# Second expert mixture: one bias product per tile of split weights in place of four bias products

## What is computed

```python
def _L1_ffn_ref(x, gate_w, expert_w, expert_b):
    gate_logits = jnp.einsum('bsd,ed->bse', x, gate_w)
    topk_vals, topk_idx = jax.lax.top_k(gate_logits, 2)
    weights = jax.nn.softmax(topk_vals.astype(jnp.float32), axis=-1)
    dense_w = jnp.sum(jax.nn.one_hot(topk_idx, E) * weights[..., None], axis=2)
    out = jnp.zeros(x.shape[:2] + (O,), dtype=x.dtype)
    for e in range(E):
        y_e = jnp.einsum('bsd,od->bso', x, expert_w[e]) + expert_b[e]
        out = out + dense_w[..., e:e + 1] * y_e
    return out

x = x + jnp.tanh(g_ffn[1]) * _L1_ffn_ref(_layernorm(x), gate_w, expert_w, expert_b)
```

## Time and profile before

| | us |
|---|---|
| median of three runs | 1305.46 (1303.05 to 1307.54) |
| the profiled execution | 1305.35 |
| its span in the trace | 1303.5 |
| TensorE busy | 1064.0 (82%) |
| VectorE busy | 840.9 (65%) |
| ScalarE busy | 545.8 (42%) |
| GpSimd busy | 530.7 (41%) |
| mean granted TensorE clock | 0.936 of full |

### The profile page before, as it was taken

The page is one execution under the profiler, slowest core; times in us unless marked ns, Lnnn a source line. Parts: engine busy times, 40 slices in busy tenths (PEclk is TensorE's granted clock), DMA queues, the critical chain, the costliest instruction groups (busy, mean ns, idle before and its releaser), DMA issues.

```text
span 1303.5 us, 32812 instructions
## 1 busy us (share of the span) xinstructions
PE 1064.0 (82%) x11717; PEld 826.4 (63%) x11717; DVE 840.9 (65%) x2315; ACT 545.8 (42%) x1065; POOL 530.7 (41%) x1053
## 2 busy tenths in 40 slices
PE   4898898994686488887888799999946569978898
PEld 2576676773576244444666577777734459977798
DVE  2565675765454689985666567777656666655475
ACT  2454465554454377664000023333311554346532
POOL 2454554654884888721101112222152224520261
PEclk8898898998798599998999899999968999989999
DMA  5321323411565554441000000000010530134331
GB/s 181 130 83 71 131 92 131 161 41 42 169 208 165 141 145 142 136 120 65 1 1 0 16 26 25 16 24 21 4 41 0 165 117 33 66 103 151 117 113 63
DMA packets 105787, 112.66 MB, mean 86 GB/s; under 512 B 12548, under 2 KB 95636, under 8 KB 104892
## 3 DMA queue, kind: packets, MB, share of 16 engines
q1 hardware_dynamic: 96732, 88.47, 21.6%
q0 software_dynamic: 8064, 22.06, 5.5%
q10 hardware_dynamic: 864, 0.43, 0.1%
HBM read 66.07 MB, written 44.84 MB: 85 GB/s over the span
## 4 chain that ended last, share of the span: by engine, by line
PE 58%; DVE 14%; issue 9%; ACT 7%; DMA 6%; POOL 5%; SPq 1%; DVEq 1%; ACTq 0%; POOLq 0%
PE psum L2677 5%; DMA PT<-xs 4%; PE psum L1082 3%; DVE mx L852 2%; PE psum L2392 2%; ACT PT L2335 2%; PE psum L1014 2%; ACT ext L2344 2%; POOL rstd L757 2%; PE psum L1065 2%; PE psum L1681 2%; PE psum L1016 2%; PE psum L1045 2%; PE psum L2377 2%; PE psum L1683 2%
## 5 line engine op out<-in xcount | busy, mean ns | idle before, releaser
L755 POOL TENSOR_SCALAR veps<-mv 128x1 f32<-128x1 f32 x112 | 27.2, 243 | 314.8 <-DVE mv L742 179.3
L852 DVE TENSOR_REDUCE mx<-psum 128x6 f32<-128x960 f32 (+3 forms) x80 | 80.7, 1009 | 68.7 <-PE psum L1050 67.4
L733 POOL DMA_INDIRECT got<-ys,rows_y x64 | 64.1, 1001 | 115.6 <-DMA ys<-yt 93.3
L939 ACT ACTIVATE PT<-psum 128x1024 f32<-128x1024 f32 x64 | 65.5, 1024 | 70.2 <-PE psum L1070 70.2
L2295 DVE TENSOR_REDUCE mx<-psum 128x4 f32<-128x1024 f32 x64 | 77.0, 1206 | 19.9 <-PE psum L2366 19.1
L2335 ACT ACTIVATE PT<-psum 128x1024 f32<-128x1024 f32 x64 | 65.5, 1023 | 34.6 <-PE psum L2377 34.3
L2677 PE MATMUL psum<-mskp,ident_r 128*128 128x512 f32 x256 | 71.3, 415 | 9.0 <-ACT PT L2630 8.6
L2106 DVE SCALAR_TENSOR_TENSOR x<-psum,cw,x 128x256 f32 (+1 forms) x128 | 53.0, 476 | 36.2 <-PE psum L2054 36.0
L1681 PE MATMUL psum<-xnTh,w7h 128*128 128x256 f32 x256 | 74.4, 291 | 1.2 <-issue 0.7
L1683 PE MATMUL psum<-xnTh,w7l 128*128 128x256 f32 x256 | 72.4, 283 | 0.0
L1682 PE MATMUL psum<-xnTl,w7h 128*128 128x256 f32 x256 | 72.4, 283 | 0.0
(11 more groups left out here) (414 smaller groups left out, 3425.2 us busy)
## 6 DMA issues: line engine op xcount, KB each, us to landing
xs<-qpad SPq DMA_DIRECT2D x17, 1024.0 KB, 5.1
PT<-xs SPq DMA_DIRECT2D x78, 128.0 KB, 2.1
ys<-yt SPq DMA_DIRECT2D x78, 128.0 KB, 2.1
ctxT<-in_ctxT SPq DMA_DIRECT2D x48, 128.0 KB, 2.3
ext<-qscr SPq DMA_DIRECT2D x96, 64.0 KB, 2.5
w_raw<-in_w SPq DMA_DIRECT2D x16, 384.0 KB, 3.3
arena<-in_w SPq DMA_DIRECT2D x4, 1280.0 KB, 10.1
q_parts<-kscr SPq DMA_DIRECT2D x66, 64.0 KB, 2.2
```

What stands on the lines that cost most here:

```text
L733: pool.indirect_dma_start(out=dst[:, t % 4, k], out_offset=None, in_=ys[:], in_offset=bass.IndirectOffsetOnAxis(ap=rows_y[:, t, k:k + 1], ...
L852: V.tensor_reduce(mx0[:, u0:u0 + m].rearrange("p j e -> p e j"), src, axis=AX.X, op=ALU.max, negate=True).then_inc(F("mx").sem, 1)
L939: A.activation(PT[:, 1024 * r:1024 * (r + 1)], bank(6, 2), ACT.Exp).then_inc(F("p").sem, 1)
```

## The change

The bias product leaves the groups: each group of a tile is six products. The bias of all eight experts, weighted, is one product per tile. For it GpSimd splits cw into three bfloat16 parts, each three times side by side (cwp, 72 columns, four instructions in `weight_parts`, issued behind the item's L755 and L757 and ahead of those of the next item). TensorE transposes cwp for both tiles into bank 6 after group 2, ahead of the router products; ScalarE copies it to cpT (72 rows by 256) between its two front copies and its tanh. After group 3 TensorE multiplies cpT by brows (72 rows by 256: for every pair of parts the bias of eight experts, in the first 256 columns of ebias) into bank 7, one product of 256 columns per tile. VectorE adds bank 7 to both tiles of x with one TENSOR_TENSOR of 512 columns, behind the last L2106 of the item and ahead of the router steps of the next. In stage 1 nine transfers of eight rows take the place of three transfers of one row.

```diff
+        pad_at = here()
         sb("pad", [128, 896])
+        cwp = over(pad_at, "cwp", [128, 2, 2, 9, TOP_E], BF16)
+        cwr = over(pad_at + 576, "cwr", [128, 2, TOP_E])
+        cpT = over(pad_at + 640, "cpT", [72, 2 * T], BF16)
+        brows = ebias[0:72, 0:C]
...
-                    pe.wait_ge(F("acc").sem, F("acc").at(b, 4 * j - 4))
+                    pe.wait_ge(F("acc").sem, F("acc").at(b, (-5, -1, 4, 8)[j]))
...
-                            MM(o, xl, wh, start=False, stop=False)
-                        t = MM(o, ones96[:], ebias[:, 512 * j:512 * (j + 1)], start=False, stop=True)
+                            t = MM(o, xl, wh, start=False, stop=(c == NC - 1))
                     t.then_inc(F("y").sem, 1)
+                    if j == 2:
+                        pe.wait_ge(F("mparts").sem, F("mparts").at(b, 4))
+                        plain(pe)
+                        for u in range(2):
+                            t = nc.tensor.transpose(bank(6).bitcast(BF16)[0:72, T * u:T * (u + 1)], cwp[:, s, u].rearrange("p c e -> p (c e)"), identb[:])
+                        t.then_inc(F("mxT_psum").sem, 1)
+                    if j == 3:
+                        pe.wait_ge(F("mxT").sem, F("mxT").at(b, 1))
+                        plain(pe)
+                        for u in range(2):
+                            t = MM(bank(7)[:, C * u:C * (u + 1)], cpT[:, T * u:T * (u + 1)], brows, start=True, stop=True)
+                        t.then_inc(F("pv").sem, 1)
...
+            def copy_weights(b):
+                act.wait_ge(f[3, "mxT_psum"].sem, f[3, "mxT_psum"].at(b, 1))
+                nc.scalar.copy(cpT[:], bank(6).bitcast(BF16)[0:72, 0:2 * T]).then_inc(f[3, "mxT"].sem, 1)
...
+            def weight_parts(n, s):
+                M = F("mparts")
+                two = cw[:, s]
+                pool.wait_ge(F("route").sem, F("route").at(n, ROUTE_STEPS[3] - 1))
+                plain(pool)
+                P.tensor_copy(cwp[:, s, :, 0:3], bc(two.unsqueeze(2), [128, 2, 3, TOP_E])).then_inc(M.sem, 1)
+                pool.wait_ge(M.sem, M.at(n, 1))
+                plain(pool)
+                P.tensor_tensor(cwr[:], two, cwp[:, s, :, 0], ALU.subtract).then_inc(M.sem, 1)
...
+            with pool.Fori(0, NB // 4) as i:
+                for s in range(2):
+                    for u in range(2):
+                        rs(i * 4 + (2 * s + u), 2 * s + u)
+                    weight_parts(i * 2 + s, s)
...
+                    if j == 3:
+                        dve.wait_ge(F("pv").sem, F("pv").at(b, 1))
+                        dve.wait_ge(acc.sem, acc.at(b, 16))
+                        nc.vector.tensor_tensor(x[:, bass.ds(2 * b, 2)] if not isinstance(b, int) else x[:, 2 * b:2 * b + 2], bank(7).rearrange("p (u c) -> p u c", u=2),
+                                                x[:, bass.ds(2 * b, 2)] if not isinstance(b, int) else x[:, 2 * b:2 * b + 2], ALU.add).then_inc(acc.sem, 1)
...
-                for r in range(3):
-                    pool.dma_start(ebias[32 * r:32 * r + 1], escr[r:r + 1]).then_inc(eb_loaded, 16)
+                for r in range(9):
+                    pool.dma_start(ebias[8 * r:8 * r + 8, 0:C], escr[r % 3].rearrange("(e n) -> e n", e=TOP_E)).then_inc(eb_loaded, 16)
```

More of the change, by code:

```diff
@@ L374, in ff_flags @@
             names = LN + [("xnT_psum", 1, 0), ("xnT", 1, 0), ("y", {3: 4, 5: 1, 7: 8}[s], 4 if s == 7 else 0),
-                          ("acc", {3: 16, 5: 1, 7: 1}[s], {3: 8, 5: 2, 7: 2}[s])]
+                          ("acc", {3: 17, 5: 1, 7: 1}[s], {3: 8, 5: 2, 7: 2}[s])]
             if s == 5:
@@ L380, in ff_flags @@
             if s == 3:
-                names += [("route", 7, 0), ("tanh", 1, 0)]
+                names += [("route", 7, 0), ("tanh", 1, 0), ("mparts", 4, 0), ("mxT_psum", 1, 0), ("mxT", 1, 0), ("pv", 1, 0)]
             if s == 7:
@@ L2067, in front, with body @@
                 router_act(3, act, b)
+            def body(p, b, n, s, turn, turn_b):
+                if n is not None:
+                    ff_front_act(3, act, n, 1 - s)
+                copy_weights(b)
+                if n is not None:
+                    router_act(3, act, n)
             def first():
@@ L2073, in first, with s3_pool @@
                     nc.scalar.copy(w3h[:, :, 512 * j:512 * (j + 1)], w3e[:, :, 512 * j:512 * (j + 1)]).then_inc(w3_high, 1)
-            pipeline(act, first, lambda p, b, n, s, turn, turn_b: front(n, 1 - s) if n is not None else None, lambda p, s: None, n_items=NB // 2)
+            pipeline(act, first, body, lambda p, s: None, n_items=NB // 2)
+        def s3_pool(pool):
+            F = lambda n: f[3, n]
+            P = nc.gpsimd
+            rs = rstd_step(3, pool)
+            def weight_parts(n, s):
[7 more added lines that the diff above has]
+                P.tensor_tensor(cwr[:], two, cwp[:, s, :, 0], ALU.subtract).then_inc(M.sem, 1)
+                pool.wait_ge(M.sem, M.at(n, 2))
+                plain(pool)
+                P.tensor_copy(cwp[:, s, :, 3:6], bc(cwr[:].unsqueeze(2), [128, 2, 3, TOP_E])).then_inc(M.sem, 1)
+                pool.wait_ge(M.sem, M.at(n, 3))
+                plain(pool)
+                P.tensor_tensor(cwp[:, s, :, 6:9], bc(cwr[:].unsqueeze(2), [128, 2, 3, TOP_E]), cwp[:, s, :, 3:6], ALU.subtract).then_inc(M.sem, 1)
+            with pool.Fori(0, NB // 4) as i:
[3 more added lines that the diff above has]
+                    weight_parts(i * 2 + s, s)
         def s3_dve(dve):
@@ L3042, in _ @@
                     s2_pool(pool)
+                elif s == 3:
+                    s3_pool(pool)
                 elif s == 7:
@@ L3075, in _ @@
                     if s == 3:
-                        pe.wait_ge(eb_loaded, 48)
+                        pe.wait_ge(eb_loaded, 144)
                     if s == 4:
```

## The result

The changed kernel takes 1315.09 us (median of 8 runs, 1310.26 to 1319.08), the kernel before 1306.5 in the same session (8 runs, 1300.03 to 1308.87): 1.0076 times as long, with a 95% interval of 1.0054 to 1.0098. The two medians lie 8.6 us apart; the ratio, which is worked out from all the runs and not from the two medians, means 9.9 us. The profiled execution took 1315.61 us with a span of 1313.8, 10.3 more than before. Stage 3 is longer by the same 10.3: from the first transposes to the last write to x it takes 144.36 us (605.29 to 749.65), before 134.04 (607.17 to 741.21).

The account below looks back on a forecast made before the run. Stage 3 was taken as bound by a circle of VectorE and TensorE arcs, with one TensorE pause a round. From 1305.35 us, +1.2 at full clock, +8.75 and -1.7 for the clock gave 1313.6, stated as 1313.5; range 1303.5 to 1319.5.

Parts of the forecast that it names:

- The circle of two arcs: Stage 3 round: VectorE arc 7.87 us to the next transposes, then TensorE arc 8.15; products in groups 0, 1 worth nothing.
- The add: VectorE's add of bank 7, between the last L2106 and the router steps: +0.85 us a round, bounds 0.68 to 1.0.
- The split: GpSimd's split of cw, ahead of the next item's L755: +0.25 us a round, bounds 0 and 0.6.
- TensorE: Stage 3 round: four bias products off the TensorE arc, -0.95 us; added transposes of cwp +0.30, bounds 0.1 to 0.5.
- Behind the last transposes: End of stage 3, without further pauses: products removed -2.85 us, transposes +0.6, product +0.45, add +0.85, together -0.95.
- The memset: GpSimd's memset of v4 would come after L747 of the last item, no longer slowing it: -0.55 us.
- All at full clock: Stage 3 without clock effects: six rounds +2.7 us, behind the last transposes -0.95, memset -0.55; together +1.2.
- The clock: Stage 3 pauses of 3.1 us bring five low-clock stretches of 1.75 us, +8.75, less the present one, -1.7.
- (a): Rival: the clock holds in most of stage 3's longer pauses; 1304.9 us, or 1308 with one or two stretches; chance 0.20.
- (b): Rival: all seven pauses of stage 3 are followed by the low clock; 1317 us, 1323 with longer stretches; chance 0.13.
- (c): Rival: TensorE's products bound stage 3, add and split hide, all 64 bias products count; 1296 us; chance 0.08.
- (d): Rival: TensorE waits for the split or ScalarE's copy in each round; 1 us each gives 1321; chance 0.04.

Follow-up runs that it names:

- a1_fill: The changed kernel with 16 unused products of 256 columns ahead of the next item's transposes, in TensorE's pause; 1301.38 us, 0.9978 of the kernel before.
- b2_no_bias: The kernel before without its 64 bias products of stage 3, nothing in their place, bias missing from the output; 1300.86 us, 0.9982 of the kernel before.
- b3_nobias_fill: The kernel before without its 64 bias products, with eight unused products in the pause; 1295.79 us, 0.9941 of the kernel before.
- a3_split_late: The changed kernel with GpSimd's split of cw moved behind the next item's reciprocal standard deviations; 1311.7 us, 1.0058 of the kernel before.
- b0_again: The kernel before run once more as a control, nothing changed; 1302.38 us, ratio 0.9997, stage 3 132.48 us.
- c2_order_split: The kernel before with group 2 ahead of the transposes, router products after group 3, third bank pair, one 72-row bias product, late add and split; 1273.23 us, 0.9779.
- a2_add_late: The changed kernel with VectorE's bias add moved behind group 1 of the next item; 1306.27 us, 1.0015 of the kernel before.

## Why the prediction was right, point by point

The forecast was 1313.5, the time is 1315.09. Its theory, a longer wait on VectorE whose main cost is the clock, was borne out by a1_fill. That the sum comes so close is in part luck: the clock took 3.1 us more than its terms, the path at full clock 1.1 us less, and the kernel before was itself at 1306.5 in the session of the result and not at 1305.35.

**The circle of two arcs** held. b2_no_bias and b3_nobias_fill show that products in groups 0 and 1 are worth nothing and those in groups 2 and 3 their full price.

**The add**: forecast +0.85, measured +0.72. The router's first copy starts 2.30 us behind the group's first L2160 (645.02 to 647.32) instead of 1.58. The instruction takes 0.691 us, nearest to the row of L1423, and it starts 0.12 us later than the copy did before (1.70 behind the first L2160 instead of 1.58), near the 0.15 of the forecast. What the forecast had not taken off is that the copy behind it starts 0.09 before the add ends.

**The split**: forecast +0.25, measured +0.43 from cw to L760 (650.06 to 651.68, 1.62 us instead of 1.19). The four instructions are hardly longer than those of the earlier trace rows, 0.22 to 0.27; with the waits between them, about 0.18 us each, the split ends 1.65 us behind cw, and I had put 1.37. Of the 0.43 only 0.28 reached TensorE (from L760 to the transposes it is 2.20 us instead of 2.35). Before, the normalisation waits for VectorE itself, which is in group 0 until 651.25; now its second half waits for GpSimd, and 0.15 of the split lies beside group 0. a3_split_late shows the same 0.28. So +0.25 was the right size by two errors that cancel.

**TensorE**: -0.95 for the four products was right. The step from the transposes of cwp to the router products is 0.11 us, as in the earlier trace rows; from their start to group 3 it is 0.98 us, where the router products alone took 0.81 before, so they cost 0.17 and not 0.30. I had added a wait for which no row spoke. So too for the two products into bank 7: they wait for nothing and cost 0.24 us (from their start at 662.43 to the second product of the next group at 662.90 it is 0.47 us, where one product takes 0.23), and the forecast had 0.45. That is why the pause is 3.26 us and not 3.1, though the VectorE arc grew by 0.99 and not by 1.10.

**A round at full clock** is therefore +0.72 +0.28 -0.95 +0.17 = +0.22, forecast +0.45. The rounds of a1_fill are 0.10 to 0.27 longer than those of b0_again.

**Behind the last transposes**: forecast -0.95. The changed kernel takes 23.73 us there with a low stretch (725.92 to 749.65), a1_fill, which has the same products there, 22.43 without one, b0_again 22.69. So at full clock it is -0.3. What I had not seen is a new wait, in TensorE's timeline of item 7 (a1_fill has it too, 1.00 us):

```profile
739.83 0.39 PE L2058 MATMUL psum<-w3h,xnTl 128*128 128x512 f32 x1
741.22 0.50 PE L2056 MATMUL psum<-w3h,xnTh 128*128 128x512 f32 x1 [1.00 <-DVE x L2160]
```

With no transposes and no pause between groups 1 and 2, TensorE reaches group 2 before VectorE has emptied the banks of group 0; VectorE begins with them only at 739.51, behind the add and the router steps.

**The memset** went as forecast. It now starts at 741.01, long behind the normalisation of item 7. The last round of a1_fill is 0.57 us shorter than that of b0_again, where the others are 0.10 to 0.27 longer.

**All at full clock**: forecast +1.2. The stage of a1_fill is 133.09, of which some 0.5 are its fillers in the first round (13.55 us, 13.02 in the changed kernel); b0_again has 132.48. So the change is worth about +0.1, nothing that a measurement tells.

**Stage 1**: forecast nothing. Stage 3 begins at 605.29 us, at 607.17 before, within the spread of the other profiles (601.6 to 609.1), so nothing shows of the six added transfers.

**The clock**: this step failed in its count. Five low stretches were forecast, seven came. The first pause, 1.96 us, which I had left out, fell as well, and so did all six of 3.04 to 3.40. The price was forecast 1.75 and is 1.45 to 1.65 in the rounds, and 1.3 behind the last transposes. The stretch that lasted 6.8 us cost 2.7. The price is less than half of the stretch for two reasons that the rows show. At 1.2 GHz a product follows the last after 0.43 us, at 2.4 GHz after 0.23, less than twice as long:

```profile
655.65 0.63 PE L2058 MATMUL psum<-w3h,xnTl 128*128 128x512 f32 x1
656.08 0.63 PE L2056 MATMUL psum<-w3h,xnTh 128*128 128x512 f32 x1
...
657.70 0.40 PE L2058 MATMUL psum<-w3h,xnTl 128*128 128x512 f32 x1
657.93 0.39 PE L2056 MATMUL psum<-w3h,xnTh 128*128 128x512 f32 x1
```

So 3.4 us hold eight products, which take 1.84 us at full clock; the difference is 1.57. And where the stretch begins within the pause, part of it falls on no work: item 3's began 0.2 us ahead of the transposes and cost 1.45, item 7's 0.6 ahead and cost 1.3.

By the stages the clock took 10.3 less 0.1, 10.2 us beyond the one low stretch of the kernel before, and the forecast was 7.05. So the clock cost 3.1 us more than forecast, the path at full clock 1.1 less.

**The rivals.** (a), the clock holds, is refuted: it held behind none of the seven pauses. (b), which had a chance of 0.13, is what happened by the count, seven of seven; its 1317 lies 1.9 us above the time, the forecast's 1313.5 lies 1.6 below. Its price of 1.75 was too high. Beside it: the Trainium skill (TensorE: Matmul & The Clock Gate, section on HAM oscillation) tells of a loop that waits for a DMA in every pass, some 3 to 5 us, and pays for the low clock in every pass. The changed kernel agrees, seven of seven with pauses of 1.96 to 3.40 us. The pauses of 0.8 to 1.8 us of the kernel before, at which the prediction held this against the page, are shorter than those the page tells of, so they don't speak against it. (c) is refuted in the changed kernel, as TensorE pauses longer; c2_order_split shows what it takes for it to hold. (d) is refuted by the row of L2064, which has no wait.

## What to carry to other kernels

Where an engine waits once in a round, work taken off it beside the wait only lengthens the wait, and on TensorE a longer pause can bring the low clock on the products behind it; unused products in the pause are a quick test of that. Before work is added to the arc that the waiting engine waits for, look for a place beside it (a2_add_late is about 8 us faster with the same instruction). Better still is independent work in the wait itself: one group of products moved there was worth 13 us of the stage, and turned the change that had lost 10 us into one that gains 14 (107.22 instead of 120.77).

## What the runs showed of the hardware

**Pause and clock.** Over the eleven profiles of stage 3 that have pauses, pauses of up to 1.82 us were never followed by the low clock (none of 37), pauses of 2.43 us and more always (22 of 22), and of those from 1.85 to 2.40 us 12 of 15 were. In between neither the length nor the program decides it: 2.06 us fell in one execution of the kernel before and held in the next. These counts are of this stage, where TensorE is busy without a break ahead of the pause; elsewhere in the trace one of 2.4 us held. A stretch lasted 3.4 us, in two cases twice that, and began between 1.0 us ahead of the transposes and 1.3 behind them.

**A slow split beside VectorE.** In item 0 three of the four instructions of the split took 1.05, 0.97 and 0.99 us instead of 0.22, and the fourth 0.28. GpSimd's timeline there, with what VectorE did:

```profile
611.79 1.05 POOL L2114 CAST cwp<-cw 128x48 bf16<-128x48 f32 x1 [7.10 <-DVE cw L1421]
613.02 0.97 POOL L2117 TENSOR_TENSOR cwr<-cw,cwp 128x16 f32<-128x16 f32 x1 [0.18 <-POOL cwp L2114]
614.16 0.99 POOL L2120 CAST cwp<-cwr 128x48 bf16<-128x48 f32 x1 [0.17 <-POOL cwr L2117]
615.34 0.28 POOL L2123 TENSOR_TENSOR cwp<-cwr,cwp 128x48 bf16<-128x48 f32 x1 [0.18 <-POOL cwp L2120]
```

```profile
611.54 3.54 DVE L2137 TENSOR_TENSOR w3l<-arena,w3h 128x1024 fp32r<-128x1024 f32 x3
```

VectorE's three instructions with two inputs from SBUF end at 615.08, and the split is fast from there. The Trainium skill (GPSIMD Engine Reference, section 1, Specifications) names contention between the two engines at SBUF when VectorE reads two inputs from it, and the rows agree. The experiments agree too. In a1_fill and a2_add_late, where the split lies beside the same three instructions, its first three take 1.05, 0.98 and 0.99 us. In a3_split_late it comes behind them, and its four take 0.34, 0.22, 0.22 and 0.28:

```profile
620.12 0.22 POOL L2117 TENSOR_TENSOR cwr<-cw,cwp 128x16 f32<-128x16 f32 x1 [0.18 <-POOL cwp L2114]
```

It costs nothing here: L760 behind it waits for VectorE's statistics (it is idle for 0.40 us until them), and TensorE asks for cwp much later.
